# Last stage of an adaLN/FFN kernel: two more groups get x2 by a product on TensorE, and every such product goes as four of 128 columns

## The chip, the cores and the metric

The kernel runs on one core of one Trainium2 chip. The metric is the device time of one execution in microseconds (us). Before the change the median of three runs is 373.33 us (373.03 to 373.79).

## The reference, cut to what matters

x holds 64 x 32 rows (2048 tokens) of 512 columns. Two layers follow each other, and each adds to x:

```
x2 = x + L0_ffn(L0_cond(x, cond))                 # gated FFN with dequantised weights and low-rank parts
out = x2 + L1_ffn(L1_cond(x2, cond, bias))
L1_cond: grouped convolution along the 512 columns (9 taps, 4 groups) + context + bias
L1_ffn(z):
    xs = 448 / max(|z|);  ws = 448 / max(|w|)
    q = fp8(clip(z * xs));  wq = fp8(clip(w * ws))
    return (q @ wq) * (1 / xs) * (1 / ws)
```

The change is in the last step: out = x2 + scale * (q @ wq), for 16 groups of 128 tokens.

## The kernel before, in words

The 2048 tokens are 16 groups of 128 rows, and 4 tiles of 4 groups. The first 317 us compute x2, tile by tile, on TensorE mostly. Then comes the convolution of the 16 slots (`convolve`, L710 and L712: f32 matmuls of 128 columns, whose stationary operand is a slot and whose moving operand are the convolution's weights), and with it the largest magnitude, which gives the scale. From about 342 us on runs the last stage.

**The last stage.** The 16 phases of each tile are cut into steps: `STEPS` gives tile 0 the steps of 4, 6 and 6 phases, tiles 1 and 2 two steps of 8 each, tile 3 steps of 8, 6 and 2. That makes ten steps, 0 to 9. For a step, VectorE computes q, the rounded values in bf16. It rounds from t16 (L1497), adds the scaled values (L1506 or L1513) and subtracts (L1525 or L1528), which writes `q_fp8`, one of three buffers. For the steps of `BY_ACT` (1, 3, 4, 5, 7, 8) ScalarE does the scaling ahead of it (L1103, L1105). TensorE then multiplies (L870): per phase four bf16 matmuls of 32 rows and 512 columns, one for each group of the tile, each into the PSUM bank g % 8 of its group. The last step of a tile ends its four groups.

**How x2 comes in.** There are three ways, by group g:

- Groups 0 to 3 (`ACCUMULATED`): x2 was written to the output early, ScalarE moves scale * bank to SBUF, and POOL's queue adds it to the output with an accumulating DMA (L1170).
- Groups in `FUSED`: TensorE adds x2 into the bank itself. `add_input` (L850) multiplies x_nat of the group by `diag`, a diagonal matrix of one value, in f32. The value is x2's factor in units of the product, so that one scaling at the end serves both. The product starts the bank's accumulation, so it stands ahead of the first step of the group's tile. `LEAD` stands ahead of step 0, and `BEHIND_STEP` says behind which step's matmuls the others come. ScalarE then moves the bank with one scaling (L1124).
- All others: VectorE computes x_nat = bank * scale + x_nat when it moves the bank (`output`, L1536).

For a bank that an earlier tile used, TensorE waits until that group has been moved (`wait_evicted(pe, g - 8)`), in `add_input` for a fused group and ahead of the tile's first step for the others. SP's queue writes the moved groups out in the order 4 to 12, 14, 15 (L557), and ScalarE's queue writes 13 (L1126).

**Order on each engine.** TensorE: the lead product, then for each step the wait for its q, its matmuls, the products of `BEHIND_STEP`. VectorE: for each step its three operations, with the moves of tile t between them, two steps after the tile's last one (`n == last_step[t] + 2`), of tile 2 behind step 8's q, of tile 3 at the end. ScalarE: the scalings of steps 1, 3, 4, 5, then its moves in the order of groups, with step 7's scalings ahead of group 4 and step 8's ahead of group 8. VectorE's q of step n waits until TensorE is through with step n - 3.

Who does what follows from the list alone:

```
def fused(g):            return g in FUSED
def moved_by_act(g):     return fused(g) or accumulated(g)
```

Before the change 4, 5, 6, 8, 9, 12 and 13 are fused, and VectorE moves five groups: 7, 10, 11, 14, 15.

Of the kernel before, what the change touches and what calls it, by code (L numbers as in the profile page):

```python
# [13 lines left out]
P = 128  # L14
# [10 lines left out]
HC = H // P  # L25
# [21 lines left out]
CONV_BANKS = 4  # L47
LATE = GROUPS - TG
ACCUMULATED = (0, 1, 2, 3)
FUSED = (4, 5, 6, 8, 9, 12, 13)  # L50
LEAD = (4,)
BEHIND_STEP = {0: (5,), 1: (6,), 3: (8,), 4: (9,), 5: (12,), 6: (13,)}
BY_ACT = (1, 3, 4, 5, 7, 8)
ACT_BUFS = 3
BIAS_ON_PE = (14, 15)
# [28 lines left out]
def build(nc, x, cond_pack, cond_w, cond_w_rest, bias_k, gate_q, up_q, gate_s, up_s,  # L84
          lr_a, lr_b, down_q, down_s, down_a, down_b, conv_w, ctx_w, fside, ffn_w,
          batch_mask, ident_in, turned, edges, ffn_turned, bias_row, lr_b_rows, out):
    with ExitStack() as ctx:
        def sb(name, shape, dt, stack=ctx):
            return stack.enter_context(nc.sbuf_tensor(name, shape, dt))

        def sem(name):
            return ctx.enter_context(nc.semaphore(name))

        ps = ctx.enter_context(nc.psum_tensor("ps", [P, 8, 512], F32))


        x_nat = sb("x_nat", [P, GROUPS, H], F32)
# [7 lines left out]
        diag = sb("diag", [P, P], F32)  # L105
# [197 lines left out]
        add_mm, ffn_mm, o_act, o_dve = sem("add_mm"), sem("ffn_mm"), sem("o_act"), sem("o_dve")  # L303
# [46 lines left out]
        def fused(g):  # L350

            return g in FUSED

# [12 lines left out]
        def wait_evicted(engine, g):  # L366

            if moved_by_act(g):
                engine.wait_ge(o_act, evicted_before(g + 1, True))
            else:  # L370
                engine.wait_ge(o_dve, evicted_before(g + 1, False))
# [190 lines left out]
        def _(pe):  # L562
            mm = nc.tensor.matmul
# [28 lines left out]
            for o in range(S // OB):  # L592
                last = mm(ps[:, MIX_BANK, o * B:(o + 1) * B], cond_w_parts[:, o, :], att_parts[:], start=True, stop=True)
# [4 lines left out]
               start=True, stop=True).then_inc(aggb_mm, 1)  # L598
# [65 lines left out]
            def low_rank_a(c, part):  # L664

                return mm(ps[:, bank(0, 1), :], lr_a_w[:, c].rearrange("p m v r -> p (m v r)"), part[:, c, :],  # L666
                          start=c == 0 and part is x1_hi, stop=c == HC - 1 and part is x1_lo)
# [84 lines left out]
            for t in range(TILES):  # L752

                for c in range(HC):
# [11 lines left out]
                    last = low_rank_a(c, x1_lo)  # L766
# [79 lines left out]
            def add_input(g):  # L846

                if g >= 8:
                    wait_evicted(pe, g - 8)
                mm(ps[:, g % 8, :], diag[:], x_nat[:, g, :], start=True, stop=False).then_inc(add_mm, 1)  # L850

            pe.wait_ge(diag_ready, 1)
            pe.wait_ge(x2_ready, GROUPS - 1)
# [3 lines left out]
            for g in LEAD:  # L857
                add_input(g)
            for n, (t, f0, k) in enumerate(steps):
                if f0 == 0:  # L860
                    for g in range(t * TG, (t + 1) * TG):
                        if not fused(g) and g >= 8:
                            wait_evicted(pe, g - 8)
                if n == 0:
                    pe.wait_ge(ffn_laid, TG * 2 * 16)
                pe.wait_ge(q_fp8_ready, n + 1)
                for f in range(f0, f0 + k):
                    for gi in range(TG):
                        rows = slice(gi * PLACES, (gi + 1) * PLACES)
                        last = mm(ps[:, (t * TG + gi) % 8, :], q_fp8[rows, n % BUFS, (f - f0) * P:(f - f0 + 1) * P],  # L870
                                  ffn_rows[2 * f // PHASES][rows, f % (PHASES // 2), :],
                                  start=f == 0 and not fused(t * TG + gi), stop=f == PHASES - 1)
                        if f == f0 + k - 1:
                            last.then_inc(ffn_mm, 1)
                for g in BEHIND_STEP.get(n, ()):
                    add_input(g)
# [767 lines left out]
```

## Time and profile before

| | |
|---|---|
| median of three runs | 373.33 us (373.03 to 373.79) |
| profiled execution | 373.0 us, of which 371.2 us are its span |
| TensorE busy | 361.3 us, 97% of the span |
| VectorE busy | 243.1 us, 65% |
| ScalarE busy | 190.3 us, 51% |
| GpSimd busy | 78.7 us, 21% |
| mean granted clock of TensorE | 0.999 |

The span is what the rows below cover; the profiled execution's own time lies 1.8 us above its span. In the rows PE is TensorE's matmuls, PEld its weight loads, DVE VectorE, ACT ScalarE, POOL GpSimd. An f32 matmul stands as two records, each with its own weight load. A row of several instructions begins with the first start and gives the time from there to the last end, and in brackets stands the engine's idle time ahead of it with what ended it. The chain of work that ended last is followed back from the end, so its pieces are start-to-start times.

### The profile page before, as it was taken

Reading aid. Unit: us, or ns where it says so; the run is one execution under the profiler, and the core shown is the slowest. Engines: PE = TensorE matmul, PEld = TensorE weight load, DVE = VectorE, ACT = ScalarE, POOL = GpSimd, SP = SyncE. Lnnn points to the kernel's source line nnn. Section 1 sums busy time; section 2 is a strip of 40 time slices with the busy share of each in tenths; the row PEclk is TensorE's granted clock in tenths of the full one; section 3 lists DMA queues with packets and bytes.
Section 4 is the critical chain, followed back from the end, with each engine's and each line's share of the span. In section 5 each row is a group of like instructions: output and inputs, shape, how many; then the busy total and the mean of one; then the engine's idle time right before and its main releaser. Section 6 shows DMA issues by size and latency. Waiting matters only on the chain.

```text
span 371.2 us, 5798 instructions
## 1 busy us (share of the span) xinstructions
PE 361.3 (97%) x2209; PEld 301.0 (81%) x2210; DVE 243.1 (65%) x409; ACT 190.3 (51%) x345; POOL 78.7 (21%) x68
## 2 busy tenths in 40 slices
PE   7999999999999999999999999999999999998994
PEld 3777887999888879998888789988888899997331
DVE  4949989436576664265766642737888822688995
ACT  5667797202656653035555641345667510066972
POOL 4000000021222332111422241113233221142040
PEclk9999999999999999999999999999999999999999
DMA  7997693495220000222200002326000299968288
GB/s 230 344 270 245 192 299 119 152 302 87 42 44 0 0 2 1 44 42 42 44 1 2 0 0 33 52 44 155 0 3 1 65 276 279 195 153 195 85 188 267
DMA packets 82476, 41.72 MB, mean 112 GB/s; under 512 B 52417, under 2 KB 72785, under 8 KB 82321
## 3 DMA queue, kind: packets, MB, share of 16 engines
q1 hardware_dynamic: 69072, 37.70, 37.4%
q10 hardware_dynamic: 12624, 1.82, 3.1%
q0 software_dynamic: 752, 1.84, 2.8%
q8 instruction: 17, 0.28, 0.3%
q14 instruction: 11, 0.08, 0.1%
HBM read 26.55 MB, written 14.80 MB: 111 GB/s over the span
## 4 chain that ended last, share of the span: by engine, by line
PE 93%; DVE 4%; ACT 1%; issue 1%; DVEq 0%
PE ps L675 44%; PE ps L660 25%; PE ps L690 6%; PE ps L608 4%; PE ps L710 3%; PE ps L870 3%; PE ps L666 2%; PE ps L712 2%; PE ps L850 1%; PE ps L623 1%; PE ps L568 1%; DVE v_plus L1506 1%; DVE q_fp L1525 1%; DVE amax L1383 0%; DVE v_plus L1513 0%
## 5 line engine op out<-in xcount | busy, mean ns | idle before, releaser
L660 PE MATMUL ps<-down_w,h_hi 128*128 128x288 f32 (+1 forms) x352 | 76.2, 297 | 0.0
L660 PE MATMUL ps<-down_w,h_lo 128*128 128x288 f32 (+1 forms) x352 | 74.7, 293 | 0.0
L675 PE MATMUL ps<-x_hi,gate_w 128*128 128x512 f32 (+1 forms) x176 | 69.9, 397 | 0.0
L675 PE MATMUL ps<-x_lo,gate_w 128*128 128x512 f32 (+1 forms) x176 | 69.6, 396 | 0.0
L675 PE MATMUL ps<-x_hi,up_w 128*128 128x512 f32 (+1 forms) x176 | 69.6, 396 | 0.0
L675 PE MATMUL ps<-x_lo,up_w 128*128 128x512 f32 (+1 forms) x176 | 69.3, 394 | 0.0
L1146 POOL TENSOR_TENSOR h_lo<-a_buf,h_hi 128x512 fp32r<-128x512 f32 (+1 forms) x33 | 42.7, 1295 | 90.0 <-ACT h_hi L984 90.0
L660 PEld LDWEIGHTS ps<-down_w,h_hi 128*128 128x128 f32 (+1 forms) x352 | 57.2, 189 | 1.1
L660 PEld LDWEIGHTS ps<-down_w,h_lo 128*128 128x128 f32 (+1 forms) x352 | 56.1, 188 | 0.0
L1435 DVE TENSOR_TENSOR a_buf<-a_buf,b_buf 128x512 f32<-128x512 f32 (+1 forms) x44 | 49.0, 1113 | 9.2 <-ACT a_buf L1050 8.1
L1157 POOL TENSOR_TENSOR x_nat<-y_buf,x_nat 128x512 f32<-128x512 f32 x15 | 20.8, 1385 | 117.0 <-DVE y_buf L1314 117.0
L1032 ACT ACTIVATE a_buf<-ps,gate_sc 128x512 f32<-128x512 f32 (+1 forms) x44 | 30.2, 687 | 25.3 <-POOL h_lo L1146 21.9
L1426 DVE TENSOR_TENSOR b_buf<-ps,b_buf 128x512 f32<-128x512 f32 (+1 forms) x44 | 30.2, 687 | 19.1 <-ACT b_buf L1039 14.9
L1039 ACT ACTIVATE b_buf<-ps,up_sc 128x512 f32<-128x512 f32 (+1 forms) x44 | 30.2, 687 | 21.1 <-PE ps L675 20.7
L675 PEld LDWEIGHTS ps<-x_hi,up_w 128*128 128x128 f32 (+1 forms) x176 | 32.6, 185 | 8.3
L675 PEld LDWEIGHTS ps<-x_lo,up_w 128*128 128x128 f32 (+1 forms) x176 | 32.8, 186 | 8.0
L675 PEld LDWEIGHTS ps<-x_lo,gate_w 128*128 128x128 f32 (+1 forms) x176 | 32.8, 186 | 7.8
L675 PEld LDWEIGHTS ps<-x_hi,gate_w 128*128 128x128 f32 (+1 forms) x176 | 32.7, 186 | 7.9
L1314 DVE TENSOR_TENSOR y_buf<-ps,y_buf 128x512 f32<-128x512 f32 x16 | 11.1, 692 | 39.2 <-PE ps L623 39.1
L1423 DVE TENSOR_TENSOR a_buf<-ps,a_buf 128x512 f32<-128x512 f32 (+1 forms) x44 | 30.3, 688 | 8.2 <-ACT a_buf L1032 7.3
L971 ACT ACTIVATE s<-s_sum 128x64 fp32r<-128x64 f32 x16 | 4.1, 257 | 59.8 <-DVE s_sum L1297 54.8
L984 ACT ACTIVATE h_hi<-a_buf 128x512 fp32r<-128x512 f32 (+1 forms) x44 | 27.5, 625 | 8.4 <-DVE a_buf L1435 8.3
(196 smaller groups left out, 486.5 us busy)
## 6 DMA issues: line engine op xcount, KB each, us to landing
x_nat<-in_x SPq DMA_DIRECT2D x4, 1024.0 KB, 6.9
out<-x_nat SPq DMA_DIRECT2D x15, 256.0 KB, 4.5
turned<-x_nat SPq DMA_DIRECT2D x12, 256.0 KB, 3.3
x_nat<-in_down_q SPq DMA_DIRECT2D x11, 256.0 KB, 4.0
x_nat<-in_gate_q SPq DMA_DIRECT2D x10, 256.0 KB, 6.4
x_nat<-in_up_q SPq DMA_DIRECT2D x10, 256.0 KB, 6.6
edges<-zeros SPq DMA_DIRECT2D x4, 512.0 KB, 9.3
xt_own<-turned SPq DMA_DIRECT2D x6, 256.0 KB, 3.4
```

The lines of the kernel that those rows point to most:

```text
L608: last = mm(ps[:, to, (g % TG) * P:(g % TG + 1) * P], x_nat[:, g, c * P:(c + 1) * P], mix[:, g, :], start=True, stop=True)
L660: last = mm(ps[:, 4 + 2 * (j % 2) + m, 0:HALF + R], part[0:k, ic, j * P:(j + 1) * P], down_w[0:k, ic, m, :], start=first, stop=end)
L675: last = mm(ps[0:k, bank(ic, 2 * m), :], w[:, H * ic + c * k:H * ic + (c + 1) * k], part[:, c, :], start=c == 0 and part is x1_hi, stop=c ...
L690: mm(ps[0:width(ic), bank(ic, 2 * m + 1), :], lr_b4[:, m, ic * P:ic * P + width(ic)], t4[m], start=True, stop=True).then_inc(l_mm, 1)
L984: activation(h_hi[0:k, ic, :], a_buf[0:k, ic % 2, :], copy).then_inc(h_hi_ready, 1)
L1032: activation(a_buf[0:k, ic % 2, :], ps[0:k, bank(ic, 0), :], copy, scale=gate_sc[0:k, ic:ic + 1]).then_inc(ag_ready, 1)
L1039: activation(b_buf[0:k, ic % 2, :], ps[0:k, bank(ic, 2), :], copy, scale=up_sc[0:k, ic:ic + 1]).then_inc(au_ready, 1)
L1146: nc.gpsimd.tensor_tensor(h_lo[0:k, ic, :], a_buf[0:k, ic % 2, :], plain(h_hi[0:k, ic, :]), ALU.subtract).then_inc(h_lo_ready, 1)
L1157: nc.gpsimd.tensor_tensor(x_nat[:, n, :], y_buf[:, j % 2, :], x_nat[:, n, :], ALU.add).then_inc(x2_ready, 1)
L1423: v.tensor_tensor(a, ps[0:k, bank(ic, 1), :], a, ALU.add).then_inc(g_ready, 1)
L1426: v.tensor_tensor(b, ps[0:k, bank(ic, 3), :], b, ALU.add).then_inc(u_ready, 1)
L1435: v.tensor_tensor(a, a, b, ALU.mult).then_inc(h_ready, 1)
```

## The change

Groups 7 and 10 become fused: the product of 7 stands behind step 2, that of 10 behind the product of 9, after step 4. So ScalarE moves them, and VectorE moves 11, 14 and 15. And `add_input` multiplies each group's x_nat in four pieces of 128 columns, of which the first starts the bank's accumulation, in place of one matmul of 512 columns. That holds for all nine fused groups.

```
-FUSED = (4, 5, 6, 8, 9, 12, 13)
+FUSED = (4, 5, 6, 7, 8, 9, 10, 12, 13)
 LEAD = (4,)
-BEHIND_STEP = {0: (5,), 1: (6,), 3: (8,), 4: (9,), 5: (12,), 6: (13,)}
+BEHIND_STEP = {0: (5,), 1: (6,), 2: (7,), 3: (8,), 4: (9, 10), 5: (12,), 6: (13,)}
...
                 if g >= 8:
                     wait_evicted(pe, g - 8)
-                mm(ps[:, g % 8, :], diag[:], x_nat[:, g, :], start=True, stop=False).then_inc(add_mm, 1)
+                for c in range(HC):
+                    at = slice(c * P, (c + 1) * P)
+                    last = mm(ps[:, g % 8, at], diag[:], x_nat[:, g, at], start=c == 0, stop=False)
+                last.then_inc(add_mm, 1)
```

HC is 4 and P is 128.

## Rows read from the trace of the kernel before

**Rows 1.** The page: busy time by engine, and the chain by engine.
```profile
PE 361.3 (97%) x2209; PEld 301.0 (81%) x2210; DVE 243.1 (65%) x409; ACT 190.3 (51%) x345; POOL 78.7 (21%) x68
...
PE 93%; DVE 4%; ACT 1%; issue 1%; DVEq 0%
```

**Rows 2.** Windows of the last stage: busy us (count) by engine, clock, DMA share, GB/s.
```profile
342.10:350.70 8.60, 7.21 (x71) 2.34 (x70) 8.38 (x13) 8.49 (x11) 0.65 (x1) 1.00 0.40 133
350.70:366.10 15.40, 15.21 (x200) 5.63 (x200) 14.47 (x18) 10.09 (x15) 3.81 (x4) 1.00 0.82 190
366.10:371.20 5.10, 0.00 (x0) 0.00 (x0) 1.41 (x2) 1.18 (x2) 0.00 (x0) 0.90 0.68 253
```

**Rows 3.** The chain in order of time, last stage: start us, us, what.
```profile
349.50 1.24 DVE q_fp L1525
...
352.69 1.06 PE ps L850 x2
...
362.42 3.67 PE ps L870 x64
```

**Rows 4.** Timeline of VectorE, last stage: start us, us, then the instructions.
```profile
345.45 0.95 DVE L1525 SCALAR_TENSOR_TENSOR q_fp<-y_buf,v_plus 128x768 bf16<-128x768 bf16 x1
...
347.37 0.96 DVE L1528 TENSOR_TENSOR q_fp<-m,v_plus 128x768 bf16<-128x768 bf16 x1
...
356.90 0.74 DVE L1536 SCALAR_TENSOR_TENSOR x_nat<-ps,small,x_nat 128x512 f32<-128x512 f32 x1
...
363.02 1.40 DVE L1536 SCALAR_TENSOR_TENSOR x_nat<-ps,small,x_nat 128x512 f32<-128x512 f32 x2
...
364.85 0.43 DVE L1528 TENSOR_TENSOR q_fp<-m,v_plus 128x256 bf16<-128x256 bf16 x1
```

**Rows 5.** Timeline of TensorE in narrow windows, step 3 and group 8's product.
```profile
350.78 0.40 PE L870 MATMUL ps<-mix,q_fp 32*128 32x512 bf16 x4 [0.37 <-DVE q_fp L1525]
...
352.30 0.38 PE L870 MATMUL ps<-mix,q_fp 32*128 32x512 bf16 x4
352.62 0.70 PE L850 MATMUL ps<-x_nat,diag 128*128 128x512 f32 x1
...
353.15 0.59 PE L850 MATMUL ps<-x_nat,diag 128*128 128x512 f32 x1
353.67 0.40 PE L870 MATMUL ps<-ffn_late,q_fp 32*128 32x512 bf16 x4
```

**Rows 6.** The chain in order of time: eight records of a slot's convolution.
```profile
324.77 0.89 PE ps L710 x8
```

**Rows 7.** Line 710: count, duration ns min/median/max, first and last start.
```profile
L710 PE MATMUL ps<-conv_wt,x_lo x16: 275/275/275, 324.6 to 326.7; 128*128 128x128 f32 x16
```

**Rows 8.** Timeline of TensorE in narrow windows, the spread of the maxima.
```profile
340.53 0.38 PE L695 MATMUL ps<-ident,amax 128*128 128x128 f32 x1 [0.57 <-DVE amax L1481]
...
340.53 0.49 PE L695 MATMUL ps<-ident,amax 128*128 128x128 f32 x2 [0.57 <-DVE amax L1481]
```

**Rows 9.** Timeline of TensorE: lead product, steps 0, 1 and 2.
```profile
342.90 1.13 PE L850 MATMUL ps<-x_nat,diag 128*128 128x512 f32 x2 [0.69 <-POOL diag L1166]
344.44 1.04 PE L870 MATMUL ps<-mix,q_fp 32*128 32x512 bf16 x16 [0.42 <-DVE q_fp L1528]
...
346.48 1.04 PE L870 MATMUL ps<-mix,q_fp 32*128 32x512 bf16 x16
...
348.94 1.47 PE L870 MATMUL ps<-ffn_late,q_fp 32*128 32x512 bf16 x24
```

**Rows 10.** Timeline of ScalarE, last stage: its moves, and step 8's second scaling.
```profile
351.41 2.39 ACT L1124 ACTIVATE x_nat<-ps,small 128x512 f32<-128x512 f32 x4
...
355.87 1.83 ACT L1124 ACTIVATE x_nat<-ps,small 128x512 f32<-128x512 f32 x3
...
358.50 0.94 ACT L1105 ACTIVATE xt_own<-t_t,small 128x768 f32<-128x768 f32 x1
...
366.01 1.27 ACT L1124 ACTIVATE x_nat<-ps,small 128x512 f32<-128x512 f32 x2 [3.35 <-PE ps L870]
```

## Prediction, made before the changed kernel was run

> **What bounds the kernel now.** I read the page first. TensorE is busy for 97% of the span and holds 93% of the chain that ended last [rows 1]. That is an average over stages, so I read the last stage by itself, in three stretches [rows 2]. The reader is to see three different limits. From 342.10 to 350.70 VectorE works 8.38 of 8.60 us, and TensorE only 7.21. From 350.70 to 366.10 TensorE works 15.21 of 15.40 us, at a granted clock of 1.00, which is the 2.4 GHz level. From 366.10 on TensorE is done, and there are two moves by VectorE, two by ScalarE and the last transfers.
>
> The chain in order of time shows where the limit changes [rows 3]. VectorE's q of step 3 lands at 349.50 + 1.24 = 350.74, TensorE starts on it at 350.78, and from there the chain is TensorE alone: steps (L870) and products of the diagonal (L850), up to 362.42 + 3.67 = 366.09. VectorE's own rows confirm it [rows 4]: its q of the last step is there at 364.85 + 0.43 = 365.28. TensorE comes to that step's 8 matmuls at about 365.5, which is two fours of 0.217 and a tail of 0.16 (both worked out below) ahead of its end. So whatever is added on TensorE behind 350.73 moves the end, and whatever is taken off VectorE there does not.
>
> **What one product costs now.** Step 3 shows the pace [rows 5]. Its first four matmuls start at 350.78, the eighth four at 352.30, so four take 1.52 / 7 = 0.217. Without a product the next four would start at 352.30 + 0.217 = 352.52. They start at 353.67: a product between two steps costs 1.15. It has four parts. 0.10 passes before its first record (352.62). The two records start 0.53 apart, and 0.52 passes from the second to the next step. The first record lasts 0.70, the second 0.59. A record lasts 0.16 beyond its streaming (a 128-column record lasts 0.275 and the next starts 0.112 later [rows 6, 7]), so the second streams 0.43, and the first has 0.11 of something else ahead of the same 0.43, which I take for a weight load that nothing hides. What is left after the second is 0.52 - 0.43 = 0.09. So of 1.15, 0.86 is streaming, and 0.10 + 0.11 + 0.09 are entry, load and exit.
>
> **The change, part by part.** First, the form: 512 columns as four of 128. The trace has no such product of the diagonal. The nearest rows are the convolution's f32 matmuls of 128 columns: eight records, which are four matmuls, take 0.89 in the chain [rows 6], 0.112 each. In that stream each record's weight load is hidden beside the record before it. The first record of a group that starts cold is longer: in the spread of the maxima the first lasts 0.38, 0.10 more than the 0.275 of a record in the stream [rows 7, 8], and the second ends 0.49 after the first began, so it starts 0.49 - 0.275 = 0.21 behind it. I therefore price the four as 0.21 + 6 x 0.112 + (0.112 + 0.09) = 1.08 from first record to next step, against 352.62 to 353.67 = 1.05 now. Splitting costs 0.03 each and gives nothing back, since the columns are the same and entry, load and exit come once either way. The bounds: 0.89 from first record to next step, if load and exit vanish (rival one); 8 x 0.21 + 0.09 = 1.77, if no load is hidden (rival two). I take 1.08, because the convolution's row is of the same type and shape, in a stream of its own kind.
>
> What the gaps are decides between 1.08 and 0.89. The Trainium skill, TensorEngine Tiling (Array Packing), Key Properties, says that a change of tiling mode drains the engine. The steps use 32-row tiles and the product the full array, so by that rule the two gaps of 0.10 and 0.09 stay whatever the pieces are, and the sum stays at 1.08 and not at 0.89; the rows show the gaps and not their cause.
>
> Second, group 7's product, new behind step 2. Steps 1 and 2 wait for TensorE and not for their q: q lands at 345.45 + 0.95 = 346.40 and 347.37 + 0.96 = 348.33 [rows 4], and the steps start at 346.48 and 348.94, when the products of groups 5 and 6 leave the engine [rows 9]. These two grow by 0.03 each, so step 2 starts 0.06 late. Its 24 matmuls are six fours: 348.94 + 6 x 0.217 = 350.24 now, and a record could start at 350.34. With the 0.06 it starts at 350.40 and ends at 350.40 + 1.08 = 351.48. Step 3 starts then and not at 350.78: **+0.70**. Only the 0.4 us in which TensorE waited for VectorE covers part of it. The lead product (group 4) is costed at nothing: it starts at 342.90 and would be done at 343.98, and step 0, which waits for its q, starts at 344.44 [rows 9].
>
> Third, group 10's product behind that of group 9: no entry, no load, no exit, 8 x 0.112 = **+0.89**, all on the path.
>
> Fourth, the split of the products of groups 8, 9, 12 and 13: 4 x 0.03 = **+0.12**.
>
> Fifth, VectorE loses two moves of 0.7 (group 7's at 356.90, and group 10's, half of the pair at 363.02) [rows 4]. Behind 350.7 nothing on the path waits for it, so it only waits longer itself: nothing.
>
> Sixth, ScalarE gets two moves of about 0.6 [rows 10]. Group 7 comes behind 4 to 6 (355.87, 1.83 for three) and ahead of step 8's two scalings, which now end at 358.50 + 0.94 = 359.44. They would end near 361 (0.6 for the move, 0.7 for the later step 4). VectorE then needs two operations of some 0.95, to 363, and TensorE now comes to step 8 at 365.5 - 6 x 0.217 = 364.2, and later with the change. Group 10 comes behind 8 and 9, where ScalarE now idles 3.35 us before groups 12 and 13. Nothing, with 1 to 3 us of cover; without it each would cost its 0.6. The waits move with the moves: product 10 needs bank 2, which ScalarE has emptied by 351.41 + 2.39 = 353.80; steps 7 to 9 need bank 7, which ScalarE would empty near 359.0 (355.87 + 0.7 + 4 x 0.61), 3 us ahead of step 7 (362.42). SP's queue writes groups 4 to 11 in order. The output of group 7 goes up to 1 us later, but that of 8, queued behind it, waits for step 6 anyway. POOL's queue holds groups 0 to 3 alone. No DMA is added.
>
> Sum: 0.70 + 0.89 + 0.12 = **+1.71**. The tail behind TensorE (5.1 us) is the same instructions and the same four last transfers. The profiled execution took 373.0 and would take 374.7; it lies 0.3 below the median of 373.33, on which I forecast **375.0**. If the split were neutral, the sum would be 0.61 + 0.86 = 1.47, or 374.8.
>
> **Rivals.** *One: the four pieces take 0.89 in all,* the load and the exit gone. For it: the chain's 0.89 for four 128-column matmuls against 1.06 for one product [rows 3, 6]. Against it: those 0.89 lie in the middle of a stream. Steps 1 and 2 would come 0.08 and 0.25 early, product 7 would run from 350.09 to 350.98 (+0.20), 10 would add 0.89, and four products would give back 0.16 each: +0.45, 373.8. *Two: the loads are not hidden,* because the four pieces load the same diagonal again and again, each record taking 0.21 as the cold pair did [rows 8]. Each product then costs 0.72 more: step 0 +0.23, steps 1 and 2 +0.95 and +1.67, step 3 at 350.34 + 1.67 + 1.77 = 353.78 (+3.00), group 8 0.72, 9 and 10 0.72 + 1.68, 12 and 13 1.44: +7.6, 380.9. Against it: 0.112 in all of the convolution's rows. The Trainium skill, TensorE: Matmul & The Clock Gate, Back-to-back issue gap, gives a sustained 81 ns for a matmul of 128 columns with its load; a record here has two passes, so by the page it would take 0.16 and the time would be some 378 (an estimate). The convolution's 0.112, 56 ns a pass, does not agree with it. *Three, on the other side: VectorE sets the end,* and two moves fewer give back 2 x 0.7 = 1.4: 371.9. It decides if TensorE has idle time behind 350.73 that waits for VectorE and takes in the two products. Against it: TensorE's idle time there is 0.19 in 15.40 us [rows 2].
>
> **How the numbers follow.** Forecast 0.78, rival one 0.12, rival two 0.05, rival three 0.05. The forecast's own cases run from 374.6 to 375.7 with the spread of runs. The range is 373.8 to 375.8: it takes in rival one and leaves out two and three. A measurement of this kernel can tell about 0.2%, or 0.75 us, from no change. Rival three is faster (0.05), rival one within 0.2% (0.12), the forecast and rival two slower (0.83).
>
> **What would show it.** Right: the first four of step 3 near 351.5; eight records of L850 per product about 0.11 apart, the second 0.21 behind the first, and gaps of 0.1 on either side; sixteen in a row behind step 4, taking 0.9 more than eight; VectorE idle by 1 us or more between 351 and 366; the same 5.1 us behind TensorE's end. Wrong: a product that leaves TensorE in 0.9, records 0.16 or 0.21 apart, or TensorE waiting for q after 351.5.

## The result, and the profile after

The changed kernel takes 375.09 us (374.74 to 375.19) against 373.33, a ratio of 1.0046 with a 95% interval of 1.0036 to 1.0056. It is 1.76 us slower; the forecast was 375.0.

The page of the changed kernel, busy time and chain by engine, against [rows 1]:

```profile
PE 363.7 (97%) x2267; PEld 307.6 (82%) x2268; DVE 242.1 (65%) x407; ACT 191.7 (51%) x347; POOL 78.7 (21%) x68
...
PE 94%; DVE 3%; DMA 1%; DVEq 0%; issue 0%; SPq 0%; ACT 0%
```

VectorE has two instructions and 1.0 us less, ScalarE two instructions and 1.4 us more, TensorE 58 matmul records and 2.4 us more. The chain's share moved from VectorE to TensorE. The middle stretch and the tail of the changed kernel's last stage, with the columns of [rows 2]:

```profile
350.70:366.10 15.40, 15.40 (x212) 9.52 (x212) 13.70 (x16) 11.57 (x17) 3.81 (x4) 1.00 0.76 164
368.10:373.30 5.20, 0.00 (x0) 0.00 (x0) 1.41 (x2) 1.21 (x2) 0.00 (x0) 0.74 0.64 240
```

The first row is the one to read: TensorE now works 15.40 of 15.40 us, and VectorE has come down from 14.47 to 13.70. The bound engine got the work, and the other one got the idle time. The second row is the tail, 5.20 where it was 5.10.

Two executions do not reach the last stage at the same moment: the lead product starts at 343.19 here and at 342.90 before [rows 9]. Up to there the two programs do the same, so I count times of the last stage from that start. The lead product by TensorE's timeline, then the chain of the changed kernel, last stage (start us, us, what), against [rows 3]:

```profile
343.19 1.16 PE L852 MATMUL ps<-x_nat,diag 128*128 128x128 f32 x8 [0.69 <-POOL diag L1169]
```
```profile
343.90 0.70 DVE q_fp L1531
...
350.77 1.09 PE ps L852 x8
351.86 1.84 PE ps L873 x32
...
356.62 1.98 PE ps L852 x16
...
364.46 3.67 PE ps L873 x64
```

TensorE is on the chain from step 0's q on, not from step 3's. Group 7's product (350.77) fills the place where TensorE waited for VectorE. A product takes 1.09 from its first record to the next step (it was 1.06), and the two behind step 4 take 1.98, so the second costs 0.89. TensorE ends at 364.46 + 3.67 = 368.13, which is 24.94 behind the lead product; before, it was 366.09 - 342.90 = 23.19. The difference is +1.75.

One product of the changed kernel in narrow windows of TensorE's timeline, against [rows 5]:

```profile
350.39 0.38 PE L873 MATMUL ps<-ffn_late,q_fp 32*128 32x512 bf16 x4
350.70 0.38 PE L852 MATMUL ps<-x_nat,diag 128*128 128x128 f32 x1
...
350.70 0.49 PE L852 MATMUL ps<-x_nat,diag 128*128 128x128 f32 x2
...
351.79 1.91 PE L873 MATMUL ps<-mix,q_fp 32*128 32x512 bf16 x32
```

It has the shape of the cold pair in [rows 8]: the first record lasts 0.38, and the second ends 0.49 after the first began. From the first record to the next step it is 351.79 - 350.70 = 1.09. The gap ahead is 350.70 - 350.39 - 0.217 = 0.09, where it was 0.10.

The engines that got and lost moves, from the timelines of VectorE and ScalarE (group 11's move, the last step's q; groups 4 to 7, step 8's second scaling):

```profile
363.58 0.75 DVE L1539 SCALAR_TENSOR_TENSOR x_nat<-ps,small,x_nat 128x512 f32<-128x512 f32 x1 [0.64 <-PE ps L873]
...
364.75 0.42 DVE L1531 TENSOR_TENSOR q_fp<-m,v_plus 128x256 bf16<-128x256 bf16 x1
```
```profile
356.65 2.42 ACT L1127 ACTIVATE x_nat<-ps,small 128x512 f32<-128x512 f32 x4 [0.38 <-PE ps L873]
...
359.86 0.95 ACT L1108 ACTIVATE xt_own<-t_t,small 128x768 f32<-128x768 f32 x1
```

VectorE now waits 0.64 for TensorE ahead of group 11, and the last q lands at 365.17, over 2 us before TensorE comes to it (its end at 368.13 less two fours of 0.217 and 0.16 is 367.54); before the change the cover was 0.2 (365.28 against some 365.5). ScalarE's four moves run one behind another, and step 8's scalings end at 360.81. VectorE's addition of step 8 begins at 360.91, right behind the scalings, so there was no cover left between these two; but the q that comes of it lands at 361.99 + 0.95 = 362.94, some 3 us before TensorE comes to step 8 (366.13). TensorE waits for neither engine.

### The profile page after: what moved, and what is told of

Read it like the earlier page. It is cut to its first block, busy times and chain, and to the rows that moved or that the text cites. A ratio compares the mean times of both kernels' runs of the same rounds, so it can differ in the third digit from the quotient of the medians.

```text
span 373.3 us, 5912 instructions
## 1 busy us (share of the span) xinstructions
PE 363.7 (97%) x2267; PEld 307.6 (82%) x2268; DVE 242.1 (65%) x407; ACT 191.7 (51%) x347; POOL 78.7 (21%) x68
## 4 chain that ended last, share of the span: by engine, by line
PE 94%; DVE 3%; DMA 1%; DVEq 0%; issue 0%; SPq 0%; ACT 0%
PE ps L675 44%; PE ps L660 25%; PE ps L690 6%; PE ps L873 4%; PE ps L608 4%; PE ps L710 3%; PE ps L852 2%; PE ps L666 2%; PE ps L712 2%; PE ps L623 1%; DMA cond_w_left<-in_cond_w_rest 1%; DVE amax L1386 0%; DVE att_bias L1211 0%; DVE cond_w_parts L1188 0%; DVEq L87 0%
```

## The experiments

The table gives TensorE's end (the end of the chain's last piece on it; for group 9 by VectorE, which has none, the end of its last row and the same 0.11) counted from the start of the lead product, and its difference to the kernel before. The last two columns are the timed runs, each against the runs of the kernel before that were made beside it. The experiments were timed in five rounds; the one with eight pieces ran once.

| kernel | TensorE's end - lead | difference | median, against before | ratio, 95% interval |
|---|---|---|---|---|
| before | 366.09 - 342.90 = 23.19 | | | |
| changed | 368.13 - 343.19 = 24.94 | +1.75 | +1.76 | 1.0046 (1.0036 to 1.0056) |
| pieces alone | 366.46 - 343.14 = 23.32 | +0.13 | +0.20 | 1.0007 (0.9995 to 1.0020) |
| whole products | 367.82 - 343.15 = 24.67 | +1.48 | +1.39 | 1.0042 (1.0029 to 1.0054) |
| group 7 alone | 367.29 - 343.25 = 24.04 | +0.85 | +0.99 | 1.0032 (1.0019 to 1.0044) |
| group 10 alone | 367.22 - 343.01 = 24.21 | +1.02 | +1.05 | 1.0036 (1.0023 to 1.0048) |
| moves alone | 366.39 - 343.19 = 23.20 | +0.01 | +0.07 | 0.9998 (0.9987 to 1.0008) |
| products in pairs | 365.77 - 342.97 = 22.80 | -0.39 | -0.26 | 0.9999 (0.9983 to 1.0016) |
| eight pieces | 371.51 - 343.25 = 28.26 | +5.07 | +5.03 | |
| pairs, last q first | 365.73 - 343.15 = 22.58 | -0.61 | -0.38 | 0.9988 (0.9979 to 0.9997) |
| the same, group 9 by VectorE | 365.20 - 342.94 = 22.26 | -0.93 | -0.45 | 0.9989 (0.9980 to 0.9998) |

**The pieces alone.** The groups stay as before.

```
-                mm(ps[:, g % 8, :], diag[:], x_nat[:, g, :], start=True, stop=False).then_inc(add_mm, 1)
+                for c in range(HC):
+                    at = slice(c * P, (c + 1) * P)
+                    last = mm(ps[:, g % 8, at], diag[:], x_nat[:, g, at], start=c == 0, stop=False)
+                last.then_inc(add_mm, 1)
```

> Groups as before; only the form of the seven products changes, from 512 columns to four of 128. Theory (columns stream alike, one load and one switch either way): each product is 0.03 us longer; those of groups 5 and 6 are covered by TensorE's wait for step 3's q, those of 8, 9, 12 and 13 count: +0.14 us, that is no measurable change, and step 3 still starts at 350.8 after an idle 0.3. Rival one (the pieces save the load and the exit, 0.16 each): -0.64 us. Rival two (loads in series): about +6 us.

The timeline of TensorE: step 3, the product behind it and the start of step 4:

```profile
351.02 1.91 PE L873 MATMUL ps<-mix,q_fp 32*128 32x512 bf16 x32 [0.30 <-DVE q_fp L1528]
352.86 1.16 PE L852 MATMUL ps<-x_nat,diag 128*128 128x128 f32 x8
353.95 0.40 PE L873 MATMUL ps<-ffn_late,q_fp 32*128 32x512 bf16 x4
```

TensorE still waits 0.30 ahead of step 3 (0.37 before), so the products of groups 5 and 6 are covered. From 352.86 to 353.95 it is 1.09, so a product is 0.03 to 0.04 longer. TensorE ends 0.13 later, as expected. The timed runs cannot tell 0.13 from no change, but they exclude the 6 us of rival two. The trace excludes rival one: splitting saves nothing.

**Whole products.** The changed kernel's groups and order, with the line of before in `add_input`.

> The changed kernel's groups and order, with each product as one matmul of 512 columns. Theory: the pieces are not what costs; the two more products are. Group 7 delays step 3 by 0.61, group 10 adds 0.86: +1.5 us on the kernel before, 0.25 us under the changed kernel. Rival one (pieces are cheaper): slower than the changed kernel, by about 1.2 us. Rival three (VectorE sets the end): faster than before.

+1.48 on TensorE where 1.47 had been worked out, and 0.27 under the changed kernel there. The chain has the pair at 1.91 and a single product at 1.06 or 1.05. What costs is the two products, and the pieces add the rest.

**Group 7 alone and group 10 alone,** both in pieces.

```
-FUSED = (4, 5, 6, 7, 8, 9, 10, 12, 13)
-BEHIND_STEP = {0: (5,), 1: (6,), 2: (7,), 3: (8,), 4: (9, 10), 5: (12,), 6: (13,)}
+FUSED = (4, 5, 6, 7, 8, 9, 12, 13)
+BEHIND_STEP = {0: (5,), 1: (6,), 2: (7,), 3: (8,), 4: (9,), 5: (12,), 6: (13,)}
```
```
-FUSED = (4, 5, 6, 7, 8, 9, 10, 12, 13)
-BEHIND_STEP = {0: (5,), 1: (6,), 2: (7,), 3: (8,), 4: (9, 10), 5: (12,), 6: (13,)}
+FUSED = (4, 5, 6, 8, 9, 10, 12, 13)
+BEHIND_STEP = {0: (5,), 1: (6,), 3: (8,), 4: (9, 10), 5: (12,), 6: (13,)}
```

> In pieces, with only group 7 added behind step 2; group 10 stays with VectorE. Theory: step 3 starts 0.70 late, and four products behind it are 0.03 longer: +0.85 us. What step 2's slack covers is seen as TensorE's idle time ahead of step 3 going from 0.37 to nothing. Rival three: VectorE's move of 0.7 at 356.9 is gone and gives back up to 0.7.

> In pieces, with only group 10 added behind group 9's product; group 7 stays with VectorE. Theory: eight records of 0.112 in a row with the eight of group 9, no second switch or load: +0.89 and +0.14 for the form: +1.03 us. Together with the run of group 7 alone the two add up to the whole change plus one +0.14. If the second product paid a switch and a load of its own, it would be +1.2 us.

The chains around the added product and at TensorE's end, group 7 alone and then group 10 alone:

```profile
349.42 1.41 PE ps L873 x24
350.83 1.09 PE ps L852 x8
351.92 1.84 PE ps L873 x32
...
363.62 3.67 PE ps L873 x64
```
```profile
349.61 1.24 DVE q_fp L1528
...
350.89 1.91 PE ps L873 x32
...
355.72 1.98 PE ps L852 x16
...
363.55 3.67 PE ps L873 x64
```

With group 7, step 2 passes to the product and the product to step 3, with no wait. With group 10, the wait for step 3's q is still there, and the pair takes 1.98, so the second product pays no entry and no load. TensorE's end moves by 0.85 and 1.02. Less the 0.13 of the form, which both hold, that is 0.85 + 1.02 - 0.13 = 1.74 against 1.75 for the whole change: the terms add up.

**The moves alone.** VectorE moves three groups and ScalarE 7 and 10, with no product for these two.

```
-FUSED = (4, 5, 6, 8, 9, 12, 13)
+FUSED = (4, 5, 6, 7, 8, 9, 10, 12, 13)
+NO_PRODUCT = (7, 10)
...
-                        if not fused(g) and g >= 8:
+                        if (not fused(g) or g in NO_PRODUCT) and g >= 8:
...
-                                  start=f == 0 and not fused(t * TG + gi), stop=f == PHASES - 1)
+                                  start=f == 0 and (not fused(t * TG + gi) or t * TG + gi in NO_PRODUCT), stop=f == PHASES - 1)
```

> VectorE moves three groups and ScalarE moves 7 and 10, as in the change, but there is no product for 7 and 10, and the other seven products stay whole: the outputs of groups 7 and 10 lack x2. Theory: VectorE's two moves and ScalarE's two lie beside TensorE's work, so taking them off VectorE is worth nothing: 0.0 us, at most 0.2 either way, and TensorE's start of step 3 and its end stay where they were. Rival three (VectorE sets the end): -1.4 us.

The lead product by TensorE's timeline, then the chain's last piece on TensorE:

```profile
343.19 1.13 PE L851 MATMUL ps<-x_nat,diag 128*128 128x512 f32 x2 [0.69 <-POOL diag L1167]
```
```profile
362.71 3.67 PE ps L871 x64
```

+0.01 on TensorE, whose end is where the chain's next piece begins (366.39), and no change in the timed runs. The 1.4 us taken off VectorE are worth nothing here, and the two moves given to ScalarE cost nothing. Rival three falls with this run alone.

**Products in pairs.** If entry, load and exit belong to the change between a step and a product, products that stand together share them. The products are whole, group 7 is fused, 10 is not.

```
-FUSED = (4, 5, 6, 8, 9, 12, 13)
-LEAD = (4,)
-BEHIND_STEP = {0: (5,), 1: (6,), 3: (8,), 4: (9,), 5: (12,), 6: (13,)}
+FUSED = (4, 5, 6, 7, 8, 9, 12, 13)
+LEAD = (4, 5)
+BEHIND_STEP = {0: (6, 7), 3: (8, 9), 5: (12, 13)}
```

> Whole products of eight groups (7 added, 10 not), set in pairs: 4 and 5 ahead of step 0, 6 and 7 behind step 0, 8 and 9 behind step 3, 12 and 13 behind step 5. Theory: a pair pays one entry, one load and one exit, so a second product costs 0.86 and not 1.15; the four products ahead of step 3 fit before its q (step 2 starts near 349.0, step 3 at 350.8 as before), and the two pairs behind it save 0.3 each: -0.6 us, 372.7. Without that saving by pairs (the gaps belong to each product): no change behind step 3, and step 3 about 0.6 late: +0.6 us or more. Rival three: faster by the move of group 7 too.

Its chain from step 3's q on:

```profile
349.57 1.24 DVE q_fp L1525
...
350.86 1.91 PE ps L870 x32
352.76 1.91 PE ps L850 x4
354.68 3.56 PE ps L870 x64
358.24 1.91 PE ps L850 x4
360.16 4.86 PE ps L870 x88
...
365.06 0.72 PE ps L870 x8
```

One more product than before, and step 3 still starts when its q is there: group 7's product found room ahead of it. A pair takes 1.91; two single products take 2 x 1.06 and a second gap of 0.10 ahead, 2.22. Step 8 starts 363.55 - 342.97 = 20.58 behind the lead product, 0.6 earlier than before (364.09 - 342.90 = 21.19), as expected. But the last eight matmuls stand by themselves, and TensorE ends only 0.39 earlier. This is the miss of the run: 0.2 us were given back ahead of step 9. VectorE's q of that step lands at 364.57 + 0.42 = 364.99, behind its moves of groups 10 and 11. In the timed runs the gain lies within the interval.

**The last q first.** To tell what held step 9, VectorE computes its q ahead of the two moves.

```
-                if n == len(steps) - 2:
-                    output(TILES - 2)
+            output(TILES - 2)
             output(TILES - 1)
```

> The kernel with the products in pairs, and VectorE computes the last step's q ahead of its moves of groups 10 and 11, not behind them. There, TensorE gained 0.6 up to step 8 and gave 0.2 back ahead of step 9, whose q lands at 364.99. Theory: VectorE's two moves (1.3) held that q; without them it lands near 363.7, TensorE no longer waits, and its end is 0.6 earlier than in the kernel before: -0.6 us, 372.8. If the wait was another's (ScalarE's, a bank's), step 9 still starts 0.2 late: -0.4 us.

Its chain, and VectorE's timeline at the end:

```profile
360.33 5.40 PE ps L870 x96
```
```profile
363.44 0.42 DVE L1528 TENSOR_TENSOR q_fp<-m,v_plus 128x256 bf16<-128x256 bf16 x1
363.78 1.40 DVE L1536 SCALAR_TENSOR_TENSOR x_nat<-ps,small,x_nat 128x512 f32<-128x512 f32 x2
365.79 1.41 DVE L1536 SCALAR_TENSOR_TENSOR x_nat<-ps,small,x_nat 128x512 f32<-128x512 f32 x2 [0.61 <-PE ps L870]
```

The q lands at 363.86, the steps 6 to 9 are one piece of 96 matmuls, and TensorE ends 0.61 earlier: VectorE's two moves had held step 9. The median is 372.90, a ratio of 0.9988 with an interval that ends at 0.9997, so this version is just clear of the kernel before, by about 0.4 us, and faster than the changed one by more. The interval reaches to 0.8 us, so the timed runs alone cannot tell 0.4 from the 0.6 that TensorE gained; the traces can: the span ends 371.1 - 365.73 = 5.4 behind TensorE's end, where it was 371.2 - 366.09 = 5.1. The windows behind TensorE's end show where the rest went, first before, then this kernel (DMA share and GB/s are the last two columns):

```profile
366.10:367.10 1.00, 0.00 (x0) 0.00 (x0) 0.95 (x2) 1.00 (x2) 0.00 (x0) 1.00 0.63 240
367.10:368.10 1.00, 0.00 (x0) 0.00 (x0) 0.46 (x1) 0.18 (x1) 0.00 (x0) 1.00 0.56 209
368.10:369.10 1.00, 0.00 (x0) 0.00 (x0) 0.00 (x0) 0.00 (x0) 0.00 (x0) 1.00 1.01 371
```
```profile
366.10:367.10 1.00, 0.00 (x0) 0.00 (x0) 1.00 (x2) 0.82 (x2) 0.00 (x0) 1.00 1.05 404
367.10:368.10 1.00, 0.00 (x0) 0.00 (x0) 0.10 (x1) 0.00 (x0) 0.00 (x0) 1.00 1.03 393
```

Before, the transfers had room when the last four groups came, and were full only from 368.10 on. Here the DMA engines are full all the while, at some 400 GB/s. VectorE's last move ends at 365.79 + 1.41 = 367.20 and the span 3.9 later, where it was 371.2 - 366.15 - 1.41 = 3.6. The likely reading is that the outputs of groups 10 and 11, which VectorE now moves later, are still under way: SP's queue issues them at 364.55 and 365.21, 1.2 and 0.5 us ahead of TensorE's end, and before at 363.79 and 364.45, 2.3 and 1.6 us ahead of it. No run took them away.

**Group 9 by VectorE too.** One product less behind step 3 (`FUSED` without 9, `BEHIND_STEP` with 3: (8,)).

> The same with group 9 taken from TensorE and moved by VectorE with 10 and 11, so TensorE has one product less behind step 3. Theory: TensorE ends some 0.4 to 0.9 earlier still (step 5 waits for its q near 355.9), but VectorE then has three moves behind step 9's q and comes to groups 14 and 15 late, so that the last move ends about where it did: -0.6 us, as with the pairs, with TensorE no longer last. If TensorE still sets the end: -1.0 to -1.4 us.

Step 5 by TensorE's timeline, then the end of the chain:

```profile
355.97 1.91 PE L870 MATMUL ps<-mix,q_fp 32*128 32x512 bf16 x32 [0.35 <-DVE q_fp L1525]
```
```profile
359.79 3.60 PE ps L870 x64
363.39 1.81 DVE x_nat L1536 x3
...
365.35 0.74 DVE x_nat L1536
```

TensorE ends 0.93 earlier than before, and VectorE's moves are now the end of the chain. That is only 0.32 earlier than with group 9 on TensorE, though a second product in a pair costs 0.85: step 5 now waits for its q from VectorE. The median is 372.83, against 372.90 no difference. So with the products in pairs, group 7's among them, and the last q ahead of the moves, there are some 0.4 us to be had from the kernel before, and then VectorE's moves (by the chain) and, as it seems, the output transfers (by the windows) set the end.

**Eight pieces of 64 columns,** groups as before, to see what paces the records.

> Groups as before; each product as eight matmuls of 64 columns. A record then streams 0.053 us, half of before, but still loads the same 128 columns of weights. If records in a row are paced by the longer of load and streaming, they come 0.11 apart whatever their width below 128, a product takes 1.9 us and not 1.05, and the time is about +5 us (step 3 at 352.4, then four times 0.88). If they are paced by streaming, 0.056 apart, a product takes 1.1 us and the time changes by +0.2 at most.

Line 852 of that kernel; one product in its chain; the first three and the first seven records of that product, by narrow windows of TensorE's timeline; and, from the trace of the kernel before, loads of 64 columns:

```profile
L852 PEld LDWEIGHTS ps<-x_nat,diag x112: 186/192/192, 343.2 to 367.5; 128*128 128x128 f32 x112
L852 PE MATMUL ps<-x_nat,diag x112: 275/275/323, 343.2 to 367.6; 128*128 128x64 f32 x112
```
```profile
354.62 1.93 PE ps L852 x16
```
```profile
354.55 0.55 PE L852 MATMUL ps<-x_nat,diag 128*128 128x64 f32 x3
...
354.55 0.99 PE L852 MATMUL ps<-x_nat,diag 128*128 128x64 f32 x7
```
```profile
L749 PEld LDWEIGHTS ps<-stage_ctx_w,cond_in_sb x4: 132/134/136, 25.4 to 25.5; 128*64 128x64 f32 x4
```

Half the columns per record, and the record still lasts 0.275. Four records more take 0.99 - 0.55 = 0.44 longer, so they come 0.11 apart, as records of 128 columns do, and the eight records more make a product 1.93 - 1.09 = 0.84 longer. The columns do not set the pace. What stayed the same is the load of 128 columns of weights for each record, and it is the likely pace: a load of 64 columns lasts 0.132 to 0.136 in the trace of before, one of 128 here 0.186 to 0.192, so 64 columns more add some 0.055, and 128 columns take some 0.11 (an estimate from these rows). No run changed the load alone. The Trainium skill, TensorE: Matmul & The Clock Gate, LDWEIGHTS (loading the stationary operand), gives a load in ns as its columns divided by 1.2, an estimate of 107 ns for 128; these rows agree with it. Of the widths run, 128 columns of f32, which stream 0.11, are the narrowest piece that costs next to nothing; no width between 64 and 128 was run.

## Why the prediction was right, point by point

- **The bound.** It was TensorE from step 3 on, as the windows had it. The moves alone show it from the other side: 1.4 us less on VectorE, no change.
- **The form.** 1.08 was predicted for a product in pieces, from the convolution's stream and the cold pair; 1.09 was measured. Entry, load and exit stayed. Rival one took a price out of the middle of a stream for the price of a piece that stands alone.
- **Group 7.** +0.70 at step 3's start: it starts 351.79 - 343.19 = 8.60 behind the lead product where it was 350.78 - 342.90 = 7.88, which is +0.72. The slack covered 0.4, and no more.
- **Group 10.** +0.89 predicted for a second product that pays no entry, load or exit; 1.98 - 1.09 = 0.89 measured.
- **The other four products.** +0.12 predicted, +0.13 for the form alone.
- **The moves and waits costed at nothing.** The named cover held: bank 7 was empty at 356.65 + 2.42 = 359.07 and step 8's scalings ended at 360.81, which less the 0.29 by which the lead product started later is 358.8 (forecast near 359.0) and 360.5 (near 361), and the last q had 2 us of slack. The tail is 5.2 and was 5.1.
- **The sum.** 1.71 predicted, 1.75 on TensorE, 1.76 in the medians. The 0.04 are 0.02 at step 3 and 0.01 in the form; the rest is within the reading. That the medians agree to 0.05 is in part luck: the runs of the changed kernel alone lie 0.45 apart.
- **Rival two** had the chance that the rows gave it: records are 0.112 apart, before in the convolution and after in the pieces (0.89 / 8 = 0.111). The Trainium skill's sustained 81 ns a matmul (TensorE: Matmul & The Clock Gate, Back-to-back issue gap), on which the prediction's 378 rested, does not agree with this case's 56 ns a pass either before or after.
- **The drain.** The runs show that the gaps belong to the change from steps to products and back: a second product behind a first costs 0.85 whole and 0.89 in pieces, which is its streaming alone. Steps and products differ in type (bf16 and f32) as well as in rows, and no run separates the two. For the exit, the trace of the kernel before does: behind the spread of the maxima an f32 record is followed by a bf16 matmul, both on the full array:

```profile
341.07 0.28 PE L695 MATMUL ps<-ident,amax 128*128 128x128 f32 x1
341.19 0.38 PE L835 MATMUL ps<-t 128*128 128x512 bf16 x1
```

The second starts 0.11 to 0.12 behind the first, the pace of records in a stream, so there is next to no gap where the type alone changes; the exit's 0.09 goes with the change of rows, or needs it. The Trainium skill's rule that a change of tiling mode drains the engine (TensorEngine Tiling (Array Packing), Key Properties) agrees with that. For the entry the traces have no such place, and it stays open whether type or rows make its 0.10.

What the prediction did not follow up lies beside the change: rival three's point, that VectorE could set the end, is near (the last q had 0.2 of cover before). With TensorE 0.6 earlier (the pairs), VectorE's last q was late at once, by 0.2.

## What to carry to other kernels

Before work is moved between engines, read which of them is idle in the very stretch from which the end is counted: here it was VectorE that had time and TensorE that had none, and both added products went to the end almost in full. Price an inserted matmul by what it does to the stream around it (gap, first load, streaming, gap), not by a record from the middle of a stream of its own kind; and put inserted matmuls of another shape side by side, where a second one costs its streaming alone.

## What the runs showed of the hardware that was not expected

A record of an f32 matmul of 64 columns lasts the same 0.275 us as one of 128 and comes the same 0.11 behind the one before, so a product in pieces of 64 took 1.93 and not 1.09; the load of each record is the likely price. And 0.6 us won on the engine that ends the chain brought some 0.4 in the time: the DMA engines were full at 393 to 404 GB/s in the two us behind TensorE's end, where before they had stood at 209 to 240 GB/s with room.
